# The squares of a segment's last states: one operation in place of two, and a strided read on TensorE

## The chip, the cores and the metric

The kernel runs on one NeuronCore of one Trainium2 chip. The metric is the device time of one execution in microseconds (us), taken over several runs; the median counts. The engines are named as the profile names them: PE (TensorE), DVE (VectorE), ACT (ScalarE), POOL (GpSimd) and SP (SyncE, here only an issuer of DMAs).

## What is computed

A block of two layers over x of shape (8, 512, 128): a state space layer (a recurrence over 512 time steps) and a mixture of experts. Only the recurrence touches the change. For each batch b, inner channel d (256) and state n (16):

```
def step(h, inp):
    dA_t, dB_t, x_t, C_t, t = inp
    h = h * dA_t + dB_t * x_t[:, :, None]
    nrm = jnp.sqrt(jnp.sum(h * h, axis=(1, 2), keepdims=True))
    fac = jnp.minimum(20.0 / (nrm + 1e-08), 1.0)
    h = jnp.where(t % 10 == 0, h * fac, h)
    y = jnp.einsum('bdn,bn->bd', h, C_t) + D_param * x_t
    return (h, y)
```

Every tenth step the state of a batch is scaled down if its norm, taken over all channels and states of that batch, is over 20. So the recurrence falls into segments of 10 steps (SEG), and between two segments stands a sum of squares over the whole state.

## The kernel before

**Layout.** The 256 channels are 2 halves of 128 partitions. A partition holds 256 rows of states (ROWS): half, then state n (together 32 values, H * NST), then batch b (8), with b innermost. A row has 11 slots (SLOT): slot 0 is the state that the segment starts from, slots 1 to 10 its ten steps. So the last state of row r lies at element 11 r + 10 of a buffer of `h`, which is a ring of three. The tile `sqb` has 256 columns in a partition for the squares of the last states. In the kernel before it is ordered batch first: 32 neighbouring columns belong to one batch.

**A segment S**, of which there are 52 (the last of 2 steps; 51 pass on a state), goes through these operations. Six segments make a window (s = 0 to 5 is the place in it); nine windows, each with side work for the windows around it (layer norm, projections, gates, the table `z` of tanh values).

- ACT, `decay` (L989): exp of the decays into PSUM, in four pieces of 82, 46, 82 and 46 rows (GRAN). Piece g + 2 reuses the PSUM of piece g, so it waits for the scan of piece g.
- POOL, `products` (L855): dB * x for the segment after this one; `c_last` (L869): product with C of the last six states of the segment before.
- DVE, `scan` (L1367): the recurrence itself, four scans, pieces of 902 and 506 elements (82 and 46 rows of 11).
- ACT, `square_last` (L999): squares of the last states in two operations. Part 0 takes rows 0 to 207 (SQROW) after the third scan, part 1 the other 48 after the fourth. Between them stands side work, mostly one or two tanh operations (`steps_tanh`, L1098).
- PE, `norm_sum` (L1699): 8 matmuls, one for a batch, with a stationary matrix of 8 columns (`sel`) and 32 moving columns of `sqb`; they add into an 8 x 32 corner of a PSUM bank. An fp32 matmul is two records in the trace, so a sum has 16.
- DVE, `take_norm` (L1335), a reduction to 8 values; POOL, `root` (L885, L887), the power -1/2; PE, `norm_spread` (L1705), which carries the 8 factors to all partitions; DVE, `restart` (L1341), which writes min(factor, 1) times the last states into slot 0 of the next segment. Only then can the first scan of the next segment run.
- DVE, `c_mult` (L1418), product with C of the first ten states; PE, `sum_y` (L1725, L1737), the sum over the states by matmuls with the identity; DVE, `gate_y` (L1352), of the segment before.

**What sets the order.** Each engine's program is written out by hand and runs in order; engines meet at semaphores. On DVE after the fourth scan stand gate_y, c_mult of four states, take_norm, c_mult of two, side work or c_mult, and restart. On ACT after the squares stand the first two decay pieces of the next segment and then tanh operations and side work up to the third piece. The semaphore `sq_done` counts squares: one at the start (L1492, by DVE), two a segment, and norm_sum k waits for 2k + 1. `square_last` part 0 also waits for the norm sum before (`nrm_done`), since it overwrites `sqb`.

Of the kernel before, what the change touches and what calls it, by code (L numbers as in the profile page):

```python
# [5 lines left out]
ALU = mybir.AluOpType  # L6
# [7 lines left out]
SEG = 10  # L14
# [7 lines left out]
RING = 3  # L22
# [13 lines left out]
def mamba_moe(nc, x, norm_w, W_in, conv_w, conv_b, W_dt, b_dt, W_B, W_C, A_log, D_param, W_out,  # L36
              residual_scale, Wg, w1, w2, out):
    B, T, DM = x.shape
    DI, NST = A_log.shape
    E, _, F = w1.shape  # L40
    H = DI // P
    RH = NST * B
    ROWS = H * RH
    NSEG = (T + SEG - 1) // SEG
# [11 lines left out]

    GRAN = [(0, 82), (82, 128), (128, 210), (210, ROWS)]
    NG = len(GRAN)
    SQROW = 208

    CP0 = 10
    CGRP = [(0, 6), (6, CP0)]
    NP = NST - CP0
# [3 lines left out]
    with ExitStack() as ctx:  # L67
        def sb(name, shape, dt=F32):
            return ctx.enter_context(nc.sbuf_tensor(name, shape, dt))

        def sem(name):
            return ctx.enter_context(nc.semaphore(name))
# [14 lines left out]
        sel = sb("sel", [P, B, B])  # L87
# [29 lines left out]
        h = sb("h", [P, RING, ROWS * SLOT])  # L117
# [4 lines left out]
        sqb = sb("sqb", [P, ROWS])  # L122
# [33 lines left out]
        ps = ctx.enter_context(nc.psum_tensor("ps", [P, 8, 512], F32))  # L156
        CBANK = (3, 4)
        YB, PA, PB = 5, 6, 7
        FCOL = H * BS
        NCOL = FCOL + B  # L160
# [5 lines left out]
        def rows(t, r):  # L166
            return t[:, r, :].rearrange("p (r c) -> p r c", c=SLOT)
# [11 lines left out]
        def region(G):  # L179

            if G % 2:
                return ps[:, 2, :]
            return ps[:, 0:2, :].rearrange("p k c -> p (k c)")

        zrow = z[:].rearrange("p (r b t) -> p r b t", r=H * NST, b=B)
        zall = z[:].rearrange("p (r t) -> p r t", t=WIN)
# [29 lines left out]
        sq_done = sem("sq_done"); nrm_done = sem("nrm_done")  # L216
# [25 lines left out]
        def place_of(S):  # L242

            return S // SPW, S % SPW
# [704 lines left out]
        def _(act):  # L949
# [7 lines left out]
            for k in range(TAPS):  # L957
                ins = act.activation(nat[:, k, :], win_n[:, 0, :], ACT.Identity, scale=conv_c[:, 0, k:k + 1])
# [17 lines left out]
            def decay(G):  # L976

                S, g = G // NG, G % NG
                w, s = place_of(S)
                if S == 0 and g < NG - 1:  # L980
                    act.wait_ge(tanh_first, g + 1)
                elif S == 0:
                    act.wait_ge(tanh_done, 1)
                elif g == 0:
                    act.wait_ge(tanh_done, 2 * w + (1 if s < HALF else 2))
                at_least(act, gscan, G - 1)
                r0, r1 = GRAN[g]
                n = LAST_STEPS - 1 if S == LS else SEG
                act.activation(region(G)[:, 0:(r1 - r0) * SLOT].rearrange("p (r c) -> p r c", c=SLOT)[:, :, 1:1 + n],  # L989
                               zall[:, r0:r1, SEG * s:SEG * s + n], ACT.Exp, scale=16.0).then_inc(exp_done, 1)  # L990

            def square_last(S, part):


                act.wait_ge(gscan, NG * S + 3 + part)
                if part == 0:
                    act.wait_ge(nrm_done, S + 1)
                r0, r1 = ((0, SQROW), (SQROW, ROWS))[part]
                act.activation(sqb[:].rearrange("p (b r) -> p r b", b=B)[:, r0 // B:r1 // B, :],  # L999
                               rows(h, S % RING)[:, r0:r1, SEG].rearrange("p (r b) -> p r b", b=B),  # L1000
                               ACT.Square).then_inc(sq_done, 1)

            def norm_x(v):
# [129 lines left out]
            for S in range(NSEG):  # L1133
                w, s = place_of(S)
                v1, v2, o = w + 1, w + 2, w - 1
                prep, ln, out_ = v1 < NWIN, v2 < NWIN, o >= 0

                if S == 0:
                    steps_tanh(0, 0, 16, 27)
                decay(NG * S + 2)  # L1140
                if S == 0:
                    steps_tanh(0, 0, 27, 32)
                decay(NG * S + 3)

                if s == 0:
                    if prep and w > 0:
                        silu_x(v1, 1)
                elif s == 1:
                    if prep:
                        half_tanh_dt(v1, 0)  # L1150
                        half_tanh_dt(v1, 1)
                elif s == 2:
                    if prep:
                        evac_bc(v1)
                    if w == 0:
                        steps_tanh(w, 1, 17, 22)
                    steps_tanh(w, 1, 28, 29)
                elif s == 3:
                    if prep:
                        tanh_gate(v1, 0)  # L1160
                        tanh_gate(v1, 1)
                    if w == NWIN - 1:
                        make_h2(o)
                    steps_tanh(v1, 0, 0, 1)
                elif s == 4:
                    if out_:
                        make_h2(o)
                elif s == 5:
                    steps_tanh(v1, 0, 24, 28)

                if S + 1 < NSEG:
                    square_last(S, 0)

                if S == 0:
                    silu_x(1, 0)
                elif s == 0:
                    steps_tanh(w, 1, 9, 10)
                elif s == 1:
                    steps_tanh(w, 1, 22, 23)
                elif s == 2:  # L1180
                    steps_tanh(w, 1, 29, 30)
                elif s == 3:
                    steps_tanh(v1, 0, 1, 3)
                elif s == 4:
                    steps_tanh(v1, 0, 14, 15)
                elif s == 5:
                    steps_tanh(v1, 0, 28, 29)

                if S + 1 < NSEG:
                    square_last(S, 1)  # L1190

                if S == 0:
                    silu_x(1, 1)
                if s == 2:
                    steps_tanh(w, 1, 30, 32)
                if s == 5:
                    steps_tanh(v1, 0, 29, 32)
                if s == 3 and ln:
                    evac_xT(v2)
                if s == (3 if w == NWIN - 1 else 4) and out_:  # L1200
                    evac_h2T(o)

                if S + 1 < NSEG:
                    decay(NG * S + 4)
                    decay(NG * S + 5)

                if S == 0:
                    steps_tanh(w, 1, 0, 12)
                elif s == 0:
                    steps_tanh(w, 1, 10, 22)  # L1210
                elif s == 1:
                    steps_tanh(w, 1, 23, 27)
                    if prep:
                        log_dt(v1)
                    steps_tanh(w, 1, 27, 28)
                    if w == 0:
                        steps_tanh(w, 1, 12, 17)
                elif s == 2:
                    if prep:
                        clamp_dt(v1)  # L1220
                    if ln:
                        norm_x(v2)
                    if prep:
                        scale_dt(v1)
                    if ln:
                        add_norm(v2)
                elif s == 3:
                    steps_tanh(v1, 0, 3, 14)
                elif s == 4:
                    steps_tanh(v1, 0, 15, 24)  # L1230
                    if ln:
                        silu_x(v2, 0)
                elif s == 5:
                    steps_tanh(v1, 1, 0, 9)
# [6 lines left out]
        def _(dve):  # L1241
# [6 lines left out]
            for q in range(2):  # L1248
                ins = dve.memset(xt[q * GRID:q * GRID + 3, :, :], 0.0)
# [196 lines left out]
            for k in range(TAPS):  # L1446
                ins = dve.tensor_scalar(nat[:, TAPS + k, :], win_n[:, 1, :], conv_c[:, 1, k:k + 1], None, ALU.mult)
# [28 lines left out]
            for G in range(2):  # L1476
                ins = dve.memset(region(G)[:, 0:(GRAN[G][1] - GRAN[G][0]) * SLOT].rearrange("p (r c) -> p r c", c=SLOT)[:, :, 0], 0.0)
# [8 lines left out]
            for hf in range(H):  # L1486
# [2 lines left out]
                                  b0b[:], ALU.mult).then_inc(pre_done, 1)  # L1489
            dve.wait_ge(pre_done, 3)  # L1490
            h_first = rows(h, 2)[:, :, 1]
            dve.tensor_tensor(sqb[:].rearrange("p (b r) -> p r b", b=B), h_first.rearrange("p (r b) -> p r b", b=B),  # L1492
                              h_first.rearrange("p (r b) -> p r b", b=B), ALU.mult).then_inc(sq_done, 1)
            make_gate(0, 0)
            make_gate(0, 1)
            take_norm(0)
# [66 lines left out]
        def _(pe):  # L1563
# [126 lines left out]

            def norm_sum(k):

                pe.wait_ge(sq_done, 2 * k + 1)
                at_least(pe, yg_done, k - 1)
                w, s = place_of(k - 1)
                if s == 5:
                    at_least(pe, lg_ready, w)
                for b in range(B):
                    ins = pe.matmul(ps[0:B, YB, NCOL:NCOL + H * NST], sel[:, b, :], sqb[:, b * H * NST:(b + 1) * H * NST],  # L1699
                                    start=(b == 0), stop=(b == B - 1))  # L1700
                ins.then_inc(nrm_done, 1)

# [42 lines left out]
            for k in range(16, 18):  # L1745
                ins = turn_w(k, nat[:, k, :])
# [129 lines left out]
```

## Time and profile before

| | us |
|---|---|
| median of 3 runs | 736.2 |
| lowest and highest | 733.01, 736.84 |
| span of the profiled execution | 732.8 |
| DVE busy in it | 579.2 (79%) |
| ACT busy in it | 581.7 (79%) |
| POOL busy in it | 591.9 (81%) |
| PE busy in it | 610.7 (83%) |

The profiled execution gives each instruction's start and duration. Its span of 732.8 us is what sums over instructions are made against; the median of the runs is 3.4 us more. The recurrence fills the span from about 36 us to about 600 us, the experts the rest. A start plus a duration is an end; durations of neighbouring instructions of an engine can overlap by about 0.1 us. In the timeline view neighbouring instructions of one line are merged (x2, x16), and idle time before them stands in brackets with what ended it.

### The profile page before, as it was taken

The page shows a single profiled execution, that of the slowest core. Times are in us where ns is not written, and L with a number is a line of the kernel's source. Part 1 is how long each engine was busy: PE and PEld are TensorE (multiplying, and loading weights), DVE is VectorE, ACT ScalarE, POOL GpSimd, SP SyncE. Part 2 cuts the span into 40 slices and gives each one's busy share as a digit, 9 for nine tenths or more (in the row PEclk, how much of TensorE's full clock was granted, in tenths as well). Part 3 has the DMA queues.
Part 4 walks back from the last instruction along what each step waited for, and adds up shares of the span by engine and source line. Part 5 has one row for each costly group of instructions (what it writes and reads, how often), then busy time and mean ns, then how long its engine had stood idle before and what let it go on. Part 6 is the DMA issues. An engine that isn't in the chain of part 4 may idle for free.

```text
span 732.8 us, 12812 instructions
## 1 busy us (share of the span) xinstructions
PE 610.7 (83%) x3988; PEld 475.9 (65%) x3988; DVE 579.2 (79%) x918; ACT 581.7 (79%) x1218; POOL 591.9 (81%) x567
## 2 busy tenths in 40 slices
PE   6698989889979889998988999898878794289774
PEld 4346667757757667766766766776667783179764
DVE  5577799899889989998998999889898982843221
ACT  4899989999998999999999999999988731233330
POOL 4488889999998989999998999998798860177774
PEclk9889899999989999999999999999988887589998
DMA  5341423245145313614542271244215202147561
GB/s 159 117 157 36 146 80 117 62 143 162 61 145 144 127 63 100 202 61 133 156 127 63 85 210 64 105 139 133 64 66 175 66 18 73 47 129 207 167 182 48
DMA packets 61735, 83.17 MB, mean 114 GB/s; under 512 B 14998, under 2 KB 47544, under 8 KB 61672
## 3 DMA queue, kind: packets, MB, share of 16 engines
q1 hardware_dynamic: 57896, 76.07, 34.0%
q0 software_dynamic: 2560, 6.08, 3.0%
q8 instruction: 30, 0.49, 0.3%
q10 hardware_dynamic: 1216, 0.27, 0.2%
q14 instruction: 33, 0.27, 0.1%
HBM read 69.81 MB, written 12.80 MB: 113 GB/s over the span
## 4 chain that ended last, share of the span: by engine, by line
ACT 27%; PE 22%; issue 17%; POOL 15%; DVE 13%; DMA 4%; POOLq 0%; SPq 0%; DVEq 0%; ACTq 0%
ACT z L1098 9%; POOL h L855 8%; DVE h L1367 7%; PE ps L1725 7%; ACT ps L989 7%; POOL h L869 4%; PE ps L1617 4%; DMA z<-rows_d,gidx 3%; PE ps L588 2%; PE ps L601 2%; ACT L1059 2%; ACT dtb L1059 1%; ACT xx L1016 1%; PE ps L1699 1%; ACT L1098 1%
## 5 line engine op out<-in xcount | busy, mean ns | idle before, releaser
L1367 DVE TENSOR_TENSOR_SCAN h<-ps,h 128x902 f32<-128x902 f32 x204 | 320.4, 1610 | 33.5 <-ACT ps L989 23.6
L855 POOL TENSOR_TENSOR h<-u,scr 128x640 f32<-128x640 f32 x208 | 298.2, 1462 | 2.4
L1725 PEld LDWEIGHTS ps<-h,ident 128*128 128x128 f32 x1632 | 239.4, 199 | 24.2 <-issue 21.8
L1725 PE MATMUL ps<-h,ident 128*128 128x160 f32 x1632 | 243.9, 310 | 3.3 <-issue 3.3
L1098 ACT ACTIVATE z<-dtb,asc 128x240 f32<-128x240 f32 x576 | 237.4, 485 | 0.3
L989 ACT ACTIVATE ps<-z 128x820 f32<-128x820 f32 (+1 forms) x208 | 138.2, 689 | 16.0 <-DVE h L1367 8.9
L869 POOL TENSOR_TENSOR h<-h,scr 128x960 f32<-128x960 f32 (+1 forms) x52 | 106.0, 2038 | 1.1 <-DVE h L1383 1.1
L1418 DVE TENSOR_TENSOR h<-h,ps 128x640 f32<-128x640 f32 (+2 forms) x169 | 106.5, 642 | 0.2
L1617 PE MATMUL ps<-xnT,wT 128*128 128x488 f32 x144 | 77.2, 652 | 0.3 <-ACT xnT L974 0.3
L1699 PE MATMUL ps<-sqb,sel 128*8 128x32 f32 x832 | 33.6, 195 | 37.6 <-ACT sqb L999 27.7
L1699 PEld LDWEIGHTS ps<-sqb,sel 128*8 128x8 f32 x832 | 27.2, 91 | 53.0 <-ACT sqb L999 45.7
L999 ACT ACTIVATE sqb<-h 128x208 f32<-128x208 f32 x102 | 44.5, 436 | 20.1 <-DVE h L1367 14.4
L1705 PEld LDWEIGHTS ps<-ident,fac 8*128 8x128 f32 x104 | 16.2, 194 | 54.1 <-POOL fac L887 52.6
L885 POOL TENSOR_TENSOR nrm<-s,guard 8x1 f32<-8x1 f32 x52 | 9.9, 190 | 46.9 <-DVE s L1335 46.9
L365 POOL DMA_INDIRECT z<-rows_d,gidx x32 | 33.2, 1039 | 15.6 <-issue 7.0
L373 POOL DMA_INDIRECT out_dram<-z,sidx x32 | 32.0, 1001 | 11.1 <-issue 9.5
L1705 PE MATMUL ps<-ident,fac 8*128 8x8 f32 x104 | 21.0, 271 | 21.8 <-POOL fac L887 20.8
L513 DVE TENSOR_SCALAR h<-ps 128x512 f32<-128x512 f32 x16 | 11.1, 692 | 35.3 <-PE ps L588 35.3
L1617 PEld LDWEIGHTS ps<-xnT,wT 128*128 128x128 f32 x144 | 26.1, 207 | 19.8 <-issue 19.2
L1341 DVE SCALAR_TENSOR_TENSOR h<-ps,h 128x256 f32<-128x256 f32 x52 | 32.0, 615 | 7.7 <-PE ps L1705 5.3
L887 POOL TENSOR_TENSOR fac<-nrm,neghalf_e 8x1 f32<-8x1 f32 x52 | 33.8, 650 | 4.1
L1637 PE MATMUL ps<-xc,wT 128*128 128x488 f32 x72 | 36.6, 620 | 0.0
(193 smaller groups left out, 820.2 us busy)
## 6 DMA issues: line engine op xcount, KB each, us to landing
scr<-b_d SPq DMA_DIRECT2D x52, 640.0 KB, 4.6
scr<-c_d SPq DMA_DIRECT2D x52, 240.0 KB, 4.4
z<-in_L_ffn_w_dram SPq DMA_DIRECT2D x32, 256.0 KB, 3.1
cdg<-cdg_d SPq DMA_DIRECT2D x52, 93.8 KB, 2.1
xx_d<-xx SPq DMA_DIRECT2D x8, 256.0 KB, 2.0
xxr<-xx_d SPq DMA_DIRECT2D x8, 256.0 KB, 2.8
rows_d<-h2b SPq DMA_DIRECT2D x16, 120.0 KB, 2.0
rows_d<-xxr SPq DMA_DIRECT2D x16, 120.0 KB, 2.3
```

The source lines that it names most:

```text
L855: pool.tensor_tensor(o.rearrange("p (n b) t -> p n b t", b=B), us.unsqueeze(1).to_broadcast([P, nn, B, SEG]), bb[:, S % RING, n0 * BS:(n0 ...
L869: pool.tensor_tensor(m, m, cc4[:, S % RING, :].rearrange("p (r t) -> p r t", t=SEG)[:, :, 0:n] .unsqueeze(1).to_broadcast([P, H, NP * B, n ...
L989: act.activation(region(G)[:, 0:(r1 - r0) * SLOT].rearrange("p (r c) -> p r c", c=SLOT)[:, :, 1:1 + n], zall[:, r0:r1, SEG * s:SEG * s + n ...
L999: act.activation(sqb[:].rearrange("p (b r) -> p r b", b=B)[:, r0 // B:r1 // B, :], rows(h, S % RING)[:, r0:r1, SEG].rearrange("p (r b) -> ...
L1098: ins = act.activation(zrow[:, k, :, t0:t1], dtb[:, v % 2, hf, :].rearrange("p (b c) -> p b c", b=B)[:, :, 1 + t0:1 + t1], ACT.Tanh, scale ...
L1367: dve.tensor_tensor_scan(hs, region(G)[:, 0:(r1 - r0) * SLOT], hs, 0.0, ALU.mult, ALU.add).then_inc(gscan, 1)
L1418: dve.tensor_tensor(m, m, ps[:, bk, c0:c0 + (n1 - n0) * BS].rearrange("p (r t) -> p r t", t=SEG)[:, :, 0:n] .unsqueeze(1).to_broadcast([P, ...
L1617: ins = pe.matmul(bankc((PA, PB)[hf]), wT[:, hf * TAPS + k, :], xnT[:, :, k:k + COLS], start=(k == 0), stop=(k == TAPS - 1))
L1637: ins = pe.matmul(bankc((PA, PB)[hf]), wT[:, 10 + hf * H + ih, :], xc[:, v % 3, ih, :], start=(ih == 0), stop=(ih == H - 1))
L1699: ins = pe.matmul(ps[0:B, YB, NCOL:NCOL + H * NST], sel[:, b, :], sqb[:, b * H * NST:(b + 1) * H * NST], start=(b == 0), stop=(b == B - 1))
L1705: pe.matmul(ps[:, YB, FCOL:FCOL + B], fac8[:, 0:1].to_broadcast([B, P]), ident[0:B, 0:B], start=True, stop=True).then_inc(fac_done, 1)
L1725: pe.matmul(ps[:, YB, 0:H * BS], ident[:], hr[:, :, n * B:(n + 1) * B, 0:SEG], start=(n == 0), stop=False)
```

## The change

`square_last` becomes one ACT operation over all 256 rows, after the fourth scan. It writes `sqb` in the order of the rows (half, state, batch), densely, in place of batch first. DVE's first square (L1492) writes in the same order. PE's `norm_sum` reads for each batch 32 columns that lie 8 elements (32 bytes) apart, in place of 32 neighbours. The semaphore count follows: one square a segment.

```
-            def square_last(S, part):
-
-
-                act.wait_ge(gscan, NG * S + 3 + part)
-                if part == 0:
-                    act.wait_ge(nrm_done, S + 1)
-                r0, r1 = ((0, SQROW), (SQROW, ROWS))[part]
-                act.activation(sqb[:].rearrange("p (b r) -> p r b", b=B)[:, r0 // B:r1 // B, :],
-                               rows(h, S % RING)[:, r0:r1, SEG].rearrange("p (r b) -> p r b", b=B),
+            def square_last(S):
+
+                act.wait_ge(gscan, NG * (S + 1))
+                act.wait_ge(nrm_done, S + 1)
+                act.activation(sqb[:], rows(h, S % RING)[:, :, SEG],
                                ACT.Square).then_inc(sq_done, 1)
...
-                if S + 1 < NSEG:
-                    square_last(S, 0)
-
...
                 if S + 1 < NSEG:
-                    square_last(S, 1)
+                    square_last(S)
...
-            dve.tensor_tensor(sqb[:].rearrange("p (b r) -> p r b", b=B), h_first.rearrange("p (r b) -> p r b", b=B),
-                              h_first.rearrange("p (r b) -> p r b", b=B), ALU.mult).then_inc(sq_done, 1)
+            dve.tensor_tensor(sqb[:], h_first, h_first, ALU.mult).then_inc(sq_done, 1)
...
-                pe.wait_ge(sq_done, 2 * k + 1)
+                pe.wait_ge(sq_done, k + 1)
...
-                    ins = pe.matmul(ps[0:B, YB, NCOL:NCOL + H * NST], sel[:, b, :], sqb[:, b * H * NST:(b + 1) * H * NST],
+                    ins = pe.matmul(ps[0:B, YB, NCOL:NCOL + H * NST], sel[:, b, :], sq_b[:, b, :],
                                     start=(b == 0), stop=(b == B - 1))
```

with `sq_b = sqb[:].rearrange("p (r b) -> p b r", b=B)`, batch first as a view of the dense tile.

How the instructions stand on ACT, in segment 5 (s = 5, the end of the first window): from the last tanh operations before the squares to the two decay pieces of the next segment. Before:

```order
L1098 ACTIVATE z<-dtb,asc 128x8x30 x4
L999 ACTIVATE sqb<-h 128x26x8
L1098 ACTIVATE z<-dtb,asc 128x8x30
L999 ACTIVATE sqb<-h 128x6x8
L1098 ACTIVATE z<-dtb,asc 128x8x30 x3
L989 ACTIVATE ps<-z 128x82x10
L989 ACTIVATE ps<-z 128x46x10
```

After:

```order
L1094 ACTIVATE z<-dtb,asc 128x8x30 x5
L996 ACTIVATE sqb<-h 128x256
L1094 ACTIVATE z<-dtb,asc 128x8x30 x3
L989 ACTIVATE ps<-z 128x82x10
L989 ACTIVATE ps<-z 128x46x10
```

The tanh operation that stood between the squares now stands ahead of them, and the 208 squares that were taken ahead of the fourth scan's end are taken behind it.

The same on ACT in a segment with s = 3, where the evacuation of a transpose (L974) stands between the squares and the decay pieces. Before:

```order
L1098 ACTIVATE z<-dtb,asc 128x8x30
L999 ACTIVATE sqb<-h 128x26x8
L1098 ACTIVATE z<-dtb,asc 128x8x30 x2
L999 ACTIVATE sqb<-h 128x6x8
L974 COPY xnT<-ps 128x512
L989 ACTIVATE ps<-z 128x82x10
L989 ACTIVATE ps<-z 128x46x10
```

After:

```order
L1094 ACTIVATE z<-dtb,asc 128x8x30 x3
L996 ACTIVATE sqb<-h 128x256
L974 COPY xnT<-ps 128x512
L989 ACTIVATE ps<-z 128x82x10
L989 ACTIVATE ps<-z 128x46x10
```

Again nothing but the squares has changed its place among the others. On PE, DVE and POOL every instruction stands where it stood; only what PE reads and what the waits count is different.

## Rows read from the trace of the kernel before

**Rows 1.** The page: busy us of each engine, share of the span, instructions.

```profile
PE 610.7 (83%) x3988; PEld 475.9 (65%) x3988; DVE 579.2 (79%) x918; ACT 581.7 (79%) x1218; POOL 591.9 (81%) x567
```

**Rows 2.** Stretch, its us, busy PE, PEld, DVE, ACT, POOL, granted clock, DMA share, GB/s.

```profile
110.00:583.00 473.00, 421.43 (x2877) 329.34 (x2877) 434.14 (x596) 446.32 (x925) 433.45 (x398) 0.96 0.38 115
```

**Rows 3.** Groups by form: out<-in, count, busy us, mean ns, idle before.

```profile
L989 ACT ACTIVATE ps<-z 128x820 f32<-128x820 f32 x102 | 86.5, 848 | 6.1 <-DVE h L1367 5.4
...
L1418 DVE TENSOR_TENSOR h<-h,ps 128x640 f32<-128x640 f32 x88 | 71.0, 807 | 0.1
L989 ACT ACTIVATE ps<-z 128x460 f32<-128x460 f32 x102 | 55.7, 546 | 3.8 <-DVE h L1367 3.5
...
L1418 DVE TENSOR_TENSOR h<-h,ps 128x320 f32<-128x320 f32 x79 | 34.9, 467 | 0.0
...
L999 ACT ACTIVATE sqb<-h 128x208 f32<-128x208 f32 x51 | 29.8, 584 | 12.4 <-DVE h L1367 11.8
...
L999 ACT ACTIVATE sqb<-h 128x48 f32<-128x48 f32 x51 | 14.8, 289 | 7.7 <-DVE h L1367 2.6
```

**Rows 4.** The same view: DVE operations that read or write with a long stride.

```profile
L1487 DVE TENSOR_TENSOR h<-u,b0b 128x128 f32<-128x128 f32 x2 | 0.6, 383 | 0.0
...
L1378 DVE TENSOR_TENSOR sqb<-h,ps 128x82 f32<-128x82 f32 x2 | 0.6, 296 | 0.3 <-ACT ps L989 0.2
...
L1378 DVE TENSOR_TENSOR sqb<-h,ps 128x46 f32<-128x46 f32 x2 | 0.4, 222 | 0.0
```

**Rows 5.** Timeline (start us, us, engine line), one segment's end, s = 1.

```profile
321.97 1.19 DVE L1367 TENSOR_TENSOR_SCAN h<-ps,h 128x506 f32<-128x506 f32 x1
322.57 0.48 ACT L1098 ACTIVATE z<-dtb,asc 128x240 f32<-128x240 f32 x1
...
323.19 0.29 ACT L999 ACTIVATE sqb<-h 128x48 f32<-128x48 f32 x1
323.29 0.81 DVE L1418 TENSOR_TENSOR h<-h,ps 128x640 f32<-128x640 f32 x1
323.38 1.31 ACT L989 ACTIVATE ps<-z 128x820 f32<-128x820 f32 x2
...
323.53 0.63 PE L1699 MATMUL ps<-sqb,sel 128*8 128x32 f32 x16 [0.43 <-ACT sqb L999]
...
324.20 0.18 DVE L1335 TENSOR_REDUCE s<-ps 8x1 f32<-8x32 f32 x1
...
324.46 0.18 POOL L885 TENSOR_TENSOR nrm<-s,guard 8x1 f32<-8x1 f32 x1 [1.11 <-DVE s L1335]
...
325.31 0.38 PE L1705 MATMUL ps<-ident,fac 8*128 8x8 f32 x2
...
325.73 0.62 DVE L1341 SCALAR_TENSOR_TENSOR h<-ps,h 128x256 f32<-128x256 f32 x1 [0.16 <-PE ps L1705]
...
326.48 3.14 DVE L1367 TENSOR_TENSOR_SCAN h<-ps,h 128x902 f32<-128x902 f32 x2
326.55 4.51 PE L1725 MATMUL ps<-h,ident 128*128 128x160 f32 x32
```

**Rows 6.** Timeline, the third scan in segments with s = 2, 3 and 4.

```profile
331.27 3.14 DVE L1367 TENSOR_TENSOR_SCAN h<-ps,h 128x902 f32<-128x902 f32 x2 [1.65 <-ACT ps L989]
...
342.81 2.04 DVE L1367 TENSOR_TENSOR_SCAN h<-ps,h 128x902 f32<-128x902 f32 x1 [0.35 <-ACT ps L989]
...
353.61 3.14 DVE L1367 TENSOR_TENSOR_SCAN h<-ps,h 128x902 f32<-128x902 f32 x2 [0.36 <-ACT ps L989]
```

**Rows 7.** Waits: us in total, times, longest us.

```profile
ACT sqb L999 <- DVE h L1367: 14.4, 34, 1.6
...
DVE s L1335 <- PE ps L1699: 5.8, 7, 1.9
```

**Rows 8.** Timeline, the segment with s = 2 of the first window.

```profile
72.59 0.55 ACT L999 ACTIVATE sqb<-h 128x208 f32<-128x208 f32 x1
...
74.42 0.18 DVE L1335 TENSOR_REDUCE s<-ps 8x1 f32<-8x32 f32 x1 [1.63 <-PE ps L1699]
```

More of the change, by code:

```diff
@@ L58, in mamba_moe @@
     NG = len(GRAN)
-    SQROW = 208
     CP0 = 10
@@ L183, in region @@
             return ps[:, 0:2, :].rearrange("p k c -> p (k c)")
+        sq_b = sqb[:].rearrange("p (r b) -> p b r", b=B)
         zrow = z[:].rearrange("p (r b t) -> p r b t", r=H * NST, b=B)
```

## The prediction, made before the changed kernel ran

> **What bounds the kernel now.** I read the busy times first. Over the whole span no engine passes 83% [rows 1], but in the stretch from 110 to 583 us, which holds most of the recurrence, DVE, ACT, POOL and PE are all busy for 89 to 94% of 473 us [rows 2], and PE has its higher clock (granted 0.96 of 2.4 GHz). With four engines that full, busy time says little; what counts is who waits for whom between two segments. So next comes the timeline around one boundary [rows 5]. The fourth scan ends at 321.97 + 1.19 = 323.16. From there:
>
> ACT's small square 323.19 to 323.48; PE's norm sum 323.53 to 324.16; DVE's reduction at 324.20; POOL's root from 324.46; PE's spread 325.31 to 325.69; DVE's restart at 325.73, after an idle 0.16 us that ended with the spread; next first scan at 326.48.
>
> DVE is not idle in between: its c_mult of four states runs from 323.29 to 324.10. So it is free 0.10 us before the sum is there. The chain square, sum, reduction and DVE's own work are matched almost to the tenth, and the reduction stands in DVE's queue ahead of the rest of c_mult, of the restart and thus of the next scan. Whatever makes the sum later makes DVE later by the same amount. The wait view agrees: only seven reductions wait noticeably longer, 5.8 us in all [rows 7].
>
> The first square, of 208 rows, is not on this path. It is taken while the fourth scan runs. ACT is early for it: it idles 12.4 us before the 51 large squares and 7.7 us before the small ones [rows 3], in 34 cases plainly waiting for a scan [rows 7].
>
> ACT is the other pacer. Where s is 2, 3 and 4 the third scan waits for an exp piece, by 1.65, 0.35 and 0.36 us [rows 6]; ACT's program from the square to that piece is then what lasts longest. In the other three kinds of segment no such wait of any size stands in the timeline.
>
> **Change 1: one square in place of two.** Before, 584 + 289 = 873 ns [rows 3]. The two sizes give a slope of (584 - 289) / 160 = 1.84 ns an element and a constant of 200 ns. The exp pieces on the same engine, whose neighbours lie in runs, have (848 - 546) / 360 = 0.84 ns. So the squares pay a full nanosecond an element for a stride. Two strides are there: the read at 44 bytes, which stays, and the write at 128 bytes, which goes. Which of them costs, ACT's rows can't say; DVE's can. Its usual product costs (807 - 467) / 320 = 1.06 ns an element plus 127 ns [rows 3]. L1378 reads at 44 bytes and writes densely: (296 - 222) / 36 = 2.06 ns. L1487 reads in runs and writes at 44 bytes: (383 - 127) / 128 = 2.0 ns [rows 4]. One stride alone, of either sort, already doubles the price. So the dense write should win little, and I take 200 + 256 x 1.84 = 671 ns. The ends: 200 + 256 x 0.84 = 415 ns if on ACT the write was the whole trouble, 873 ns if merging saves nothing.
>
> The merged square starts where the small one started, 0.03 us behind the fourth scan, and so ends 671 - 289 = 0.38 us later. On ACT the tanh operation of 0.48 us that stood between the squares [rows 5] moves ahead, into time in which ACT is now idle. ACT saves 202 ns of work but can't use them: the saving is a longer wait for the scan. What stands behind the square, the decay pieces and all up to the third piece, is 0.38 us late.
>
> The Trainium skill, "Advanced Engine Details and Errata", section "The Read-Write Bubble", advises large operations on ScalarE and VectorE, since memory latency shows as a bubble between instructions. The 200 ns that a merge saves agree with it; what the rule would make of the time is the last rival below.
>
> **Change 2: PE reads with a stride of 32 bytes.** Sixteen records take 0.63 us [rows 5]; with 193 ns for a single one they stand (0.63 - 0.19) / 15 = 29 ns apart. The state sum streams 160 columns a record, 32 records in 4.51 us, or 135 ns each [rows 5], which is 0.85 ns a column; for 32 columns that is 27 ns. So the norm sum is paced by its moving columns, not by issue, and a slower read shows in full. No matmul of the trace reads single fp32 elements with a gap. Bounds: nothing, or four times (each element fetched anew for each half pass): 16 x 0.081, about 1.25 us. Nearest are DVE's and ACT's rows, where an element with a gap costs twice one in a run; I take that, 16 x 0.027 = 0.42 us. A gain is excluded, since a dense read is the least that can be asked.
>
> The rule that speaks against this change: the Trainium skill, "Advanced Engine Details and Errata", section "SBUF Cachelines", says that SBUF has 16-byte lines, that at least two hits on a line are needed to hide the latency, and that an access to a new line each time pays. By it both strides here pay, as DVE's rows show; it gives no figure for PE.
>
> DVE's first square, once, is strided on one side instead of two: nothing. The counts on `sq_done` cost nothing. The merged square's wait for the last norm sum is met long before.
>
> **The sum.** The sum's end is late by D = 0.38 + 0.42 = 0.80 us, DVE's reduction by 0.79. How much of it is still there when the third scan of the next segment starts depends on who was waited for. Into s = 2 DVE had waited 1.65 us for ACT, so DVE's lateness is covered and ACT's own 0.38 is left. Into s = 3 and 4 the covers are 0.35 and 0.36: 0.44 and 0.43 are left. Into s = 5, 0 and 1 there is next to no cover; for two of them I take off 0.15, the idle time before the restart [rows 5], which POOL's root can hide where it was late for its own reasons: 0.79 + 0.64 + 0.64. Together 0.38 + 0.44 + 0.43 + 2.07 = 3.3 us a window, 0.55 a segment. Of the 51 segments I count 45. In some at the start, around 220 us and at the end the sum was late for another reason (PE's queue, or ACT not yet there), as in [rows 8], where the large square starts only at 72.59 and DVE then idles 1.63 us; there ACT's saved 0.2 us is even of use. 45 x 0.55 = 25 us. The profiled execution would go from 732.8 to 758; with the 3.4 us by which the median lies above it, **761 us**.
>
> PE's own 51 x 0.42 = 21 us of extra streaming are in time in which it waits for squares or roots. If that cover were gone, gate_y would wait for sum_y; I count nothing.
>
> **Rivals.**
> - PE reads the strided columns for nothing. Then both engines are 0.38 late at every boundary: 45 x 0.38 = 17, 753 us. For it: PE's records may hide a fetch that DVE can't. Chance 0.28.
> - PE's read costs four times: D = 1.63. Left are 0.38 + 1.28 + 1.27 + 1.63 + 1.48 + 1.48 = 7.5 a window, 45 x 1.25 = 56: 792 us. Chance 0.08.
> - The write stride was ACT's price, PE's read costs double: the square takes 415 ns, so ACT is 0.13 late and D is 0.55. Left: 0.13 + 0.20 + 0.19 + 0.55 + 0.40 + 0.40 = 1.9 a window, 14 in all: 750 us. Against it stand L1378 and L1487. Chance 0.09.
> - Both cheap, 415 ns and nothing on PE: 45 x 0.13 = 6, 742 us, or hardly slower at all if the constant shrinks to that of exp (160 ns) and the early segments give some back. Chance 0.06.
> - The other side: ACT's work, not its wait, sets the pace. Then 202 ns a segment come off, 51 x 0.20 = 10, 726 us. It decides only where ACT reaches the square after the fourth scan's end; [rows 3, 7] show ACT waiting, [rows 8] is one of the few exceptions. This is also what the skill's advice on large operations would bring. Chance 0.02.
>
> **How the numbers follow.** The forecast has 0.45, its own range about 754 to 767 (45 to 51 segments, covers off by a tenth). With the first and third rivals 0.82 of the chance lies between 745 and 768. What is left over, 0.02, is for something not seen. About 0.5%, 3.7 us, is what a measurement of this kernel can tell from no change: faster 0.02, same 0.04, slower 0.94.
>
> **What would show it.** The squares' row: 51 operations of 128x256, mean near 671 ns (415 would be the write stride). The norm sum's 16 records: 1.05 us (0.63: PE reads for nothing; 1.9: four times). From the fourth scan's end to the reduction 1.85 us in place of 1.04, with DVE idle about 0.9 us before it, some 45 us in all over the reductions. The third scan's waits for ACT in s = 3 and 4 nearly gone, in s = 2 about 1.2 us. ACT's idle before the squares some 0.6 us each. I am wrong if the reduction doesn't idle, or if segments with s = 2 grow as much as those with s = 5.

## The result, and the profile after

The changed kernel takes 765.8 us (median of 4 runs, 763.5 to 771.1); the kernel before, measured beside it again, 735.1. The ratio is 1.044, with a 95% interval of 1.039 to 1.048. The profiled execution went from 732.8 to 761.8 us, 29 us more.

The page: busy time of each engine in the changed kernel, to be read against [rows 1]. ACT and DVE are busy for less, PE for 34 us more, and the span is longer: the time went into waiting.

```profile
span 761.8 us, 12761 instructions
...
PE 644.3 (85%) x3988; PEld 499.9 (66%) x3988; DVE 576.8 (76%) x918; ACT 575.2 (76%) x1167; POOL 592.8 (78%) x567
```

The view of groups by form says where DVE waits (last columns: busy us, mean ns, idle us before them and what ended it). The functions are those of the kernel before, their lines a few lower: scan L1360, norm_sum L1691, square_last L996, gate_y L1345, take_norm L1328.

```profile
L1360 DVE TENSOR_TENSOR_SCAN h<-ps,h 128x902 f32<-128x902 f32 x102 | 206.6, 2026 | 20.6 <-ACT ps L989 11.7 <-POOL h L855 1.6 <-DVE h L1334 1.0
...
L1691 PE MATMUL ps<-sqb,sel 128*8 128x32 f32 x832 | 58.2, 238 | 36.0 <-ACT sqb L996 29.6 <-DVE sqb L1485 4.9 <-DVE yg L1345 0.8
...
L996 ACT ACTIVATE sqb<-h 128x256 f32<-128x256 f32 x51 | 33.7, 660 | 41.6 <-DVE h L1360 41.5
...
L1345 DVE TENSOR_TENSOR yg<-ps,sgn 128x160 f32<-128x160 f32 x51 | 15.7, 308 | 15.9 <-PE ps L1729 15.9
...
L1328 DVE TENSOR_REDUCE s<-ps 8x1 f32<-8x32 f32 x52 | 9.3, 178 | 46.0 <-PE ps L1691 45.9
```

And the same groups of the kernel before, of which the rows ahead of the prediction show only the squares.

```profile
L1367 DVE TENSOR_TENSOR_SCAN h<-ps,h 128x902 f32<-128x902 f32 x102 | 207.4, 2033 | 33.0 <-ACT ps L989 23.0 <-POOL h L855 1.6 <-DVE h L1341 1.0
...
L1699 PE MATMUL ps<-sqb,sel 128*8 128x32 f32 x832 | 33.6, 195 | 37.6 <-ACT sqb L999 27.7 <-DVE sqb L1492 4.9 <-DVE lgb L1441 4.7
...
L1352 DVE TENSOR_TENSOR yg<-ps,sgn 128x160 f32<-128x160 f32 x51 | 15.5, 305 | 8.2 <-PE ps L1737 8.2
...
L1335 DVE TENSOR_REDUCE s<-ps 8x1 f32<-8x32 f32 x52 | 9.3, 179 | 9.8 <-PE ps L1699 5.8
```

DVE idles 46.0 - 9.8 = 36.2 us longer before the reduction of the norm sum (of the 9.8 us before, 5.8 ended with PE's sum) and 15.9 - 8.2 = 7.7 us longer for the state sum, and 33.0 - 20.6 = 12.4 us less before its large scans, nearly all of it waits for ACT's exp pieces. Together 31.5, against a span that grew by 29 while DVE's busy time shrank by 2.4.

One boundary, the counterpart of [rows 5] (timeline, s = 1). The fourth scan ends at 335.56 + 3.11 = 338.67.

```profile
335.56 3.11 DVE L1360 TENSOR_TENSOR_SCAN h<-ps,h 128x902 f32<-128x902 f32 x2
...
338.71 0.66 ACT L996 ACTIVATE sqb<-h 128x256 f32<-128x256 f32 x1 [0.94 <-DVE h L1360]
338.81 0.81 DVE L1411 TENSOR_TENSOR h<-h,ps 128x640 f32<-128x640 f32 x1
...
339.42 1.12 PE L1691 MATMUL ps<-sqb,sel 128*8 128x32 f32 x16 [0.66 <-ACT sqb L996]
...
340.57 0.18 DVE L1328 TENSOR_REDUCE s<-ps 8x1 f32<-8x32 f32 x1 [0.96 <-PE ps L1691]
...
342.10 0.61 DVE L1334 SCALAR_TENSOR_TENSOR h<-ps,h 128x256 f32<-128x256 f32 x1 [0.16 <-PE ps L1697]
...
342.84 3.14 DVE L1360 TENSOR_TENSOR_SCAN h<-ps,h 128x902 f32<-128x902 f32 x2
...
347.17 3.14 DVE L1360 TENSOR_TENSOR_SCAN h<-ps,h 128x902 f32<-128x902 f32 x2 [1.19 <-ACT ps L989]
```

From the end of the scan to the reduction it is 1.90 us, where it was 1.04: the square 0.37 longer (660 ns for 289), PE's sixteen records 0.49 longer (1.12 for 0.63). DVE's c_mult ends at 339.62 and DVE then stands for 0.96 us. The restart follows the reduction by 1.53 us, as before. The third scan of the next segment (347.17), which waited 1.65 us for ACT [rows 6], waits 1.19.

From first scan to first scan, the growth of a segment in two neighbouring windows, in us:

| s | 0 | 1 | 2 | 3 | 4 | 5 | sum |
|---|---|---|---|---|---|---|---|
| segments 24 to 29 | 1.50 | 0.70 | 0.39 | 0.39 | 0.39 | 0.55 | 3.9 |
| segments 30 to 35 | 0.90 | 1.03 | 0.04 | 0.38 | 0.38 | 0.69 | 3.4 |

Segments with s = 2, 3 and 4 grow by ACT's 0.38 in both windows (once by 0.04, where the segment before took the rest). The others grow by more, and by an amount that changes from window to window; that had to be explained.

### The profile page after: what moved, and what is told of

Its sections match the earlier page's. It is cut to its first block, busy times and chain, and to the rows that moved or that the text cites. A ratio compares the mean times of both kernels' runs of the same rounds, so it can differ in the third digit from the quotient of the medians.

```text
span 761.8 us, 12761 instructions
## 1 busy us (share of the span) xinstructions
PE 644.3 (85%) x3988; PEld 499.9 (66%) x3988; DVE 576.8 (76%) x918; ACT 575.2 (76%) x1167; POOL 592.8 (78%) x567
## 4 chain that ended last, share of the span: by engine, by line
PE 32%; DVE 27%; issue 17%; ACT 12%; POOL 6%; DMA 3%; DVEq 0%; POOLq 0%; SPq 0%; ACTq 0%
DVE h L1360 15%; PE ps L1717 10%; PE ps L1691 6%; PE ps L1609 4%; DVE h L1411 3%; ACT sqb L996 3%; PE ps L1629 2%; ACT z L1094 2%; POOL fac L887 2%; ACT ps L989 2%; DVE h L1334 2%; POOL out_dram L373 2%; DMA z<-rows_d,gidx 2%; DVE bst L1260 2%; PE ps L1697 1%
## 5 line engine op out<-in xcount | busy, mean ns | idle before, releaser
L1360 DVE TENSOR_TENSOR_SCAN h<-ps,h 128x902 f32<-128x902 f32 x204 | 317.1, 1606 | 21.1 <-ACT ps L989 12.3
L1717 PEld LDWEIGHTS ps<-h,ident 128*128 128x128 f32 x1632 | 239.1, 199 | 27.2 <-issue 23.9
L1094 ACT ACTIVATE z<-dtb,asc 128x240 f32<-128x240 f32 x576 | 235.0, 485 | 0.3
L989 ACT ACTIVATE ps<-z 128x820 f32<-128x820 f32 (+1 forms) x208 | 139.9, 692 | 33.6 <-DVE h L1360 26.0
L1691 PE MATMUL ps<-sqb,sel 128*8 128x32 f32 x832 | 58.2, 238 | 36.0 <-ACT sqb L996 29.6
L1691 PEld LDWEIGHTS ps<-sqb,sel 128*8 128x8 f32 x832 | 48.7, 105 | 51.1 <-ACT sqb L996 41.9
L1609 PE MATMUL ps<-xnT,wT 128*128 128x488 f32 x144 | 79.3, 667 | 0.3 <-ACT xnT L974 0.3
L996 ACT ACTIVATE sqb<-h 128x256 f32<-128x256 f32 x51 | 33.7, 660 | 41.6 <-DVE h L1360 41.5
L1328 DVE TENSOR_REDUCE s<-ps 8x1 f32<-8x32 f32 x52 | 9.3, 178 | 46.0 <-PE ps L1691 45.9
L1629 PE MATMUL ps<-xc,wT 128*128 128x488 f32 x72 | 43.2, 714 | 0.4 <-DVE xc L1317 0.4
```

The source lines that it names most:

```text
L996: act.activation(sqb[:], rows(h, S % RING)[:, :, SEG], ACT.Square).then_inc(sq_done, 1)
L1094: ins = act.activation(zrow[:, k, :, t0:t1], dtb[:, v % 2, hf, :].rearrange("p (b c) -> p b c", b=B)[:, :, 1 + t0:1 + t1], ACT.Tanh, scale ...
L1360: dve.tensor_tensor_scan(hs, region(G)[:, 0:(r1 - r0) * SLOT], hs, 0.0, ALU.mult, ALU.add).then_inc(gscan, 1)
L1609: ins = pe.matmul(bankc((PA, PB)[hf]), wT[:, hf * TAPS + k, :], xnT[:, :, k:k + COLS], start=(k == 0), stop=(k == TAPS - 1))
L1629: ins = pe.matmul(bankc((PA, PB)[hf]), wT[:, 10 + hf * H + ih, :], xc[:, v % 3, ih, :], start=(ih == 0), stop=(ih == H - 1))
L1717: pe.matmul(ps[:, YB, 0:H * BS], ident[:], hr[:, :, n * B:(n + 1) * B, 0:SEG], start=(n == 0), stop=False)
```

## The experiments

The theory: two losses of their own, ACT's square (later for the sum and for ACT itself) and PE's strided read (later for the sum), each partly covered by the other's or by older waits. Rivals: all is PE's read; all is the merge; the two only hurt together. All ratios are to runs of the kernel before on the same chip; the chips differ by up to 2% (before: 731.7, 734.7 and 747.9 us in the three groups of runs), so only ratios are compared.

**1. Each part alone.** `merge_only`: one square, but layout and reads as before.

```
+                act.activation(sqb[:].rearrange("p (b r) -> p r b", b=B),
+                               rows(h, S % RING)[:, :, SEG].rearrange("p (r b) -> p r b", b=B), ACT.Square)
```

> Part one of the change alone: one square of 256 rows after the fourth scan, but written batch first as before, and PE reads 32 neighbours as before. Own theory (a merged square makes the boundary late whatever PE does): square about 670 ns, the norm sum's 16 records in 0.63 us, the sum 0.38 us later after the fourth scan than before, ACT late by the same, 45 x 0.38 = 17 us: about 752 us. If all the loss were in PE's strided read: as before, 735 us. If ACT's saved 0.2 us a segment counted: 725 us.

Measured: ratio 1.034 (1.031 to 1.037), 757.3 against 731.7 us. That is 25.6 us, half as much again as expected. `stride_only`: two squares at their places, written in the order of the rows, PE's strided read.

```
-                act.activation(sqb[:].rearrange("p (b r) -> p r b", b=B)[:, r0 // B:r1 // B, :],
-                               rows(h, S % RING)[:, r0:r1, SEG].rearrange("p (r b) -> p r b", b=B),
+                act.activation(sqb[:, r0:r1], rows(h, S % RING)[:, r0:r1, SEG],
```

> Part two alone: two squares at their old places, written densely in the order of the rows, and PE reads with a stride of 32 bytes. Own theory: 238 ns a record and 1.12 us a sum as in the changed kernel, so DVE's reduction 0.49 us late, ACT not late; covered in segments with s = 2, partly in s = 3 and 4 by scans that wait for ACT (0.35 us): 0 + 0.14 + 0.13 + 0.49 + 0.34 + 0.34 = 1.4 us a window, 12 us in all: about 747 us. If the merge were all of the loss: 735 us. If the two losses only hurt together (each covered alone): both this and the merge alone near 735 us.

Measured: 1.020 (1.017 to 1.023), 746.6 against 731.7, 14.9 us. Groups by form, first of the merge alone, then of the stride alone:

```profile
L1361 DVE TENSOR_TENSOR_SCAN h<-ps,h 128x902 f32<-128x902 f32 x102 | 207.2, 2032 | 34.7 <-ACT ps L989 25.3 <-POOL h L855 1.6 <-DVE h L1335 1.0
...
L996 ACT ACTIVATE sqb<-h 128x256 f32<-128x256 f32 x51 | 34.0, 667 | 48.1 <-DVE h L1361 47.9
...
L1346 DVE TENSOR_TENSOR yg<-ps,sgn 128x160 f32<-128x160 f32 x51 | 15.6, 307 | 15.7 <-PE ps L1731 15.7
...
L1329 DVE TENSOR_REDUCE s<-ps 8x1 f32<-8x32 f32 x52 | 9.3, 179 | 22.2 <-PE ps L1693 22.1
```

```profile
L1368 DVE TENSOR_TENSOR_SCAN h<-ps,h 128x902 f32<-128x902 f32 x102 | 206.8, 2027 | 23.3 <-ACT ps L991 14.4 <-POOL h L857 1.6 <-DVE h L1342 1.0
L1699 PE MATMUL ps<-sqb,sel 128*8 128x32 f32 x832 | 58.1, 238 | 25.1 <-ACT sqb L1001 16.5 <-DVE sqb L1493 4.9 <-DVE lgb L1442 3.0
...
L1336 DVE TENSOR_REDUCE s<-ps 8x1 f32<-8x32 f32 x52 | 9.3, 179 | 33.7 <-PE ps L1699 33.6
```

Both parts hurt alone, so the three rivals fall. With the merge alone the waits before the large scans stay about as long as they were (33.0 and 34.7 us), since DVE and ACT are late together. With the stride alone DVE is late and ACT is not, and they shrink to 23.3 us: part of the later sum is covered by older waits for ACT.

The parts add up to 40 us on that chip, and the change costs 4.4%, 31 to 32 us. That doesn't mean that one hides the other at the boundary, as a look at whole windows shows. Six segments last, from first scan to first scan (start of the first scan of segment 18, 24, 30 and 36), in us; in brackets gate_y's waits for the state sum in them that are over 0.15 us:

| | segments 18 to 23 | 24 to 29 | 30 to 35 |
|---|---|---|---|
| before | 64.56 | 64.56 | 64.56 |
| stride_only | 65.48 | 66.98 (0.77) | 65.48 |
| merge_only | 66.78 | 68.35 (1.50) | 68.35 (1.42) |
| act_late (experiment 3) | 66.53 | 66.72 (0.82) | 66.38 |
| merge_filled (experiment 4) | 68.86 (0.78) | 68.56 (0.49) | 66.89 |
| changed kernel | 68.89 (1.36) | 68.47 (1.10) | 67.98 (0.59) |
| after_filled (experiment 4) | 67.65 | 67.66 | 67.63 |

The lines behind two of these numbers, the windows of the merge alone from 246.66 and from 313.44 us:

```profile
246.66 2.04 DVE L1361 TENSOR_TENSOR_SCAN h<-ps,h 128x902 f32<-128x902 f32 x1
...
313.44 2.04 DVE L1361 TENSOR_TENSOR_SCAN h<-ps,h 128x902 f32<-128x902 f32 x1
...
320.97 0.33 DVE L1346 TENSOR_TENSOR yg<-ps,sgn 128x160 f32<-128x160 f32 x1 [1.08 <-PE ps L1731]
...
381.79 2.04 DVE L1361 TENSOR_TENSOR_SCAN h<-ps,h 128x902 f32<-128x902 f32 x1
```

Where gate_y doesn't wait, the stride costs 0.9 us a window, the merge 2.2 (six times 0.37) and both together 3.1: there the parts simply add up. What is not additive lies in the windows in which gate_y waits. These waits grow by 2.6 us over the span with the stride (8.2 to 10.8), by 7.5 with the merge and by 7.7 with both. That accounts for 2.4 of the missing 8 to 9 us; the rest isn't explained, and one profiled execution of each kernel doesn't tell how often such windows come in the others.

**2. Which stride costs, and from what distance.** `merge_dense_read` is the changed kernel with PE reading 32 neighbours; `read_stride_8B` and `read_stride_16B` read every second and every fourth column; `blocks_of_4` lays the squares out so that a batch has four neighbouring columns in each block of 32.

```
-                    ... sel[:, b, :], sq_b[:, b, :],
+ merge_dense_read   ... sel[:, b, :], sqb[:, b * H * NST:(b + 1) * H * NST],
+ read_stride_8B     ... sel[:, b, :], sqb[:, 0:2 * H * NST].rearrange("p (r two) -> p r two", two=2)[:, :, b % 2],
+ read_stride_16B    ... sel[:, b, :], sqb[:, 0:4 * H * NST].rearrange("p (r four) -> p r four", four=4)[:, :, b % 4],
+ blocks_of_4        ... sel[:, b, :], sqb[:].rearrange("p (q b i) -> p b q i", b=B, i=4)[:, b],
```

> The changed kernel, but PE reads 32 neighbouring columns of the row-ordered squares (so each sum takes the wrong squares, the norm is not the reference's). Against the merge alone it differs only in ACT's write, dense in place of 128 bytes apart. If the read stride alone sets ACT's price: the same square and the same time as the merge alone, within 0.3%. If a write stride adds its own price to it: square shorter here by up to 0.26 us (415 ns) and some 11 us less. PE's sum 0.63 us.

> The changed kernel, but PE reads every second column (8 bytes apart) from the first 64 (the norm is not the reference's). If the price of PE's read is one per 16-byte line with fewer than two hits: two hits a line, no price, sum 0.63 us and the time of the merge with a dense read (about 752 us). If any gap between single elements doubles the price: 1.12 us and the changed kernel's 766 us.

> The changed kernel, but PE reads every fourth column (16 bytes apart) from the first 128 (the norm is not the reference's). Theory of lines (one element in a 16-byte line costs double): 238 ns a record, 1.12 us a sum, 766 us (ratio 1.04) as with 32 bytes. If the price grew with the distance or came from the bank: between 193 and 238 ns.

> The changed kernel with another layout of the squares: blocks of 32 in which a batch has 4 neighbouring columns (one line of 16 bytes). ACT writes elements 16 bytes apart in one operation, PE reads runs of 4 with 112 bytes between the runs. Theory of lines: PE pays nothing (193 ns, 0.63 us), ACT pays no more than for its read (square 660 to 671 ns), so the time of the merge alone, ratio 1.034. If any jump cost PE something, the sum would be over 0.63 us.

| | distance of PE's columns | ns a record | ACT's square, mean ns | ratio (95%) |
|---|---|---|---|---|
| merge_only | 4 B | 195 | 667 | 1.034 (1.031 to 1.037) |
| merge_dense_read | 4 B | 195 | 660 | 1.034 (1.028 to 1.039) |
| read_stride_8B | 8 B | 194 | 660 | 1.033 (1.028 to 1.038) |
| blocks_of_4 | runs of 4, then 112 B | 195 | 675 | 1.031 (1.027 to 1.035) |
| read_stride_16B | 16 B | 237 | 660 | 1.041 (1.038 to 1.044) |
| changed kernel | 32 B | 238 | 660 | 1.044 (1.039 to 1.048) |

The norm sum of segments with s = 1, in the timeline of 8 bytes, then of 16 bytes:

```profile
331.34 0.64 PE L1691 MATMUL ps<-sqb,sel 128*8 128x32 f32 x16 [0.67 <-ACT sqb L996]
```

```profile
341.20 1.12 PE L1691 MATMUL ps<-sqb,sel 128*8 128x32 f32 x16 [0.67 <-ACT sqb L996]
```

PE's price is a step: nothing at 8 bytes, double at 16, the same double at 32, and nothing for jumps of 112 bytes between runs of four. That is what a price for having a single element in a line of 16 bytes would give; a distance of 12 bytes and other alignments were not tried. Here the rule of the Trainium skill ("Advanced Engine Details and Errata", "SBUF Cachelines": at least two hits on a 16-byte line) and the trace agree, for PE also, on which the page gives no figure: (1.12 - 0.24) / 15 = 59 ns between records of 32 columns, 29 before.

On ACT the write stride is worth 7 ns of 667, so it is not what the squares pay for. That leaves the read at 44 bytes; no run reads the squares densely, so its own price stays argued. With the order of the rows the change therefore buys ACT next to nothing and charges PE 0.49 us a segment.

**3. Is it ACT or the sum that the merge makes late?** `act_late` is the kernel before with an ACT operation on a scratch tile behind the small square (it takes 400 ns).

```
                     square_last(S, 1)
+                    act.activation(junk[:], wT[:, 0:2, :].rearrange("p k c -> p (k c)"), ACT.Identity)
```

> The kernel before with an ACT operation of 256 columns on a scratch tile right behind the small square, about 0.38 us, with no one waiting for it: ACT is as late as with the merged square, while the norm sum comes at its old time. If ACT's lateness is half of the merge's loss: growth where scans wait for ACT (s = 2, 3, 4: 0.38 us each, 45 / 6 x 1.14 = 9 us, 741 us where before is 732, ratio 1.012). If only the late sum hurts: 732 us, 1.00. If the clock falls less often here than with the merge, s = 0 and s = 3 stay without their extra 0.7 us and more.

Measured: 1.018 (1.014 to 1.021), 12.4 us, of which I had expected 9. Groups by form:

```profile
L1369 DVE TENSOR_TENSOR_SCAN h<-ps,h 128x902 f32<-128x902 f32 x102 | 207.5, 2034 | 44.8 <-ACT ps L990 35.8 <-POOL h L856 1.6 <-DVE h L1343 1.0
...
L1354 DVE TENSOR_TENSOR yg<-ps,sgn 128x160 f32<-128x160 f32 x51 | 15.6, 305 | 8.3 <-PE ps L1739 8.1
...
L1337 DVE TENSOR_REDUCE s<-ps 8x1 f32<-8x32 f32 x52 | 9.3, 179 | 9.8 <-PE ps L1701 5.9
```

All of it is in the wait for exp pieces (33.0 to 44.8 us); the reductions wait 9.8 us as ever. The added operation makes ACT late by less than its 400 ns, as the timeline of a segment with s = 1 shows:

```profile
327.47 0.29 ACT L1000 ACTIVATE sqb<-h 128x48 f32<-128x48 f32 x1
...
327.67 0.40 ACT L1192 ACTIVATE junk<-wT 128x256 f32<-128x256 f32 x1
...
327.97 1.31 ACT L990 ACTIVATE ps<-z 128x820 f32<-128x820 f32 x2
```

From the small square to the decay piece it is 0.50 us, where it was 0.19 [rows 5]: ACT is 0.31 us late, where the merge makes it 0.37 late. For that an undisturbed window pays 66.53 - 64.56 = 1.97 us and 1.82 in the next but one (table above), six times 0.30 to 0.33. So ACT's path was about last in all six kinds of segment, not in three. (In the kernel before the third scan waits for ACT by 0.02 to 0.10 us where s is 5, 0 and 1.) ACT's lateness is by itself enough for the 2.2 us that the merge costs an undisturbed window, while DVE's later sum runs beside it. In whole executions the run costs half of the merge, 12.4 of 25.6 us; the difference is mostly in windows in which gate_y waits.

**4. Why the merge costs 25 us and not 17.** Seven and a half windows (45 segments) at 2.2 us would be the 17 us that were expected. The rest is in windows in which gate_y waits: 68.35 us in place of 66.78 for the merge, where gate_y waits for 1.50. In the windows in which s = 0 grew most, PE is slow just ahead of the late gate_y. Timeline of the changed kernel around segment 24, and under it the view of stretches (the granted clock is the third number from the end):

```profile
319.97 2.00 PE L1609 MATMUL ps<-xnT,wT 128*128 128x488 f32 x2
...
321.76 1.55 PE L1629 MATMUL ps<-xc,wT 128*128 128x488 f32 x2
...
328.10 0.32 DVE L1345 TENSOR_TENSOR yg<-ps,sgn 128x160 f32<-128x160 f32 x1 [1.10 <-PE ps L1729]
```

```profile
319.50:322.90 3.40, 3.40 (x6) 1.95 (x7) 2.92 (x4) 3.18 (x10) 3.24 (x4) 0.50 0.88 232
322.90:326.30 3.40, 3.40 (x25) 3.16 (x25) 3.40 (x3) 2.94 (x5) 3.40 (x3) 1.00 0.40 119
```

The same two pairs of matmuls took 1.09 and 0.98 us before. Between 319.5 and 322.9 us the granted clock was 0.50 (the lower level, 1.2 GHz), after PE had waited 0.72 us for the square and 0.38 for the root. The state sum starts late and gate_y stands for 1.10 us. In the kernel before PE waits just as long at this place, 0.68 and 0.38 us, and the granted clock of the stretch from 305.4 to 308.8 us, which holds the same matmuls, is 1.00; so these two waits alone don't tell why the clock fell. Between 110 and 560 us the trace of the kernel before has 7 such stretches, that of the merge alone 10 (the expectation below says 6 and 12, a miscount), and in the kernel before four of the seven begin at the end of a segment with s = 2 (272, 337, 402 and 467 us), where gate_y doesn't wait. `merge_filled` gives PE a matmul nobody needs ahead of the norm sum; `after_filled` and `before_filled` do it to the changed kernel and to the kernel before.

```
+                if s != 1 and w < NWIN - 1 and S > 2:
+                    pe.matmul(ps[:, CBANK[1], 0:256], ones_w[:], wT[:, 0:2, :].rearrange("p k c -> p (k c)"),
+                              start=True, stop=True)
                 norm_sum(S + 1)
```

> The merge alone plus a matmul of 256 columns (about 0.45 us) on PE right ahead of the norm sum, into a free PSUM bank, in all segments from the fourth on but s = 1 and the last window; its result isn't used. With the merge alone PE's clock is at its lower level in 12 stretches between 110 and 560 us, in the kernel before in 6, and segments with s = 0 and s = 3 grow by 1.2 and 1.0 us in place of 0.4 in the windows in which the clock falls. If these falls are PE's longer idle times and cost time: fewer lower stretches and about 7 us less than the merge alone (ratio 1.024). If the extra growth has another cause: the ratio stays 1.034 or goes up, since the filler delays the sum where PE is not idle for 0.45 us.

> The changed kernel plus the same filler on PE ahead of the norm sum (256 columns, about 0.45 us, result unused). The filler took about 8 us (1.1%) off the merge alone. In the changed kernel the waits of gate_y for the state sum (15.9 us against 8.2 before) stood where PE's clock had fallen. If the fallen clock makes them: gate_y's waits near 10 us, and a ratio to before of about 1.034 in place of 1.044. If PE is simply too full with the slower reads: the filler adds work, 1.044 or more.

> The kernel before plus the same filler. There PE idles only 0.4 to 1.0 us ahead of the sum, so the filler delays the sum a little where the idle time is shorter than 0.45 us. If the clock's falls in the kernel before (granted 0.97 between 110 and 560 us) cost anything on the path: up to 3 us faster, ratio 0.996. If they lie where PE has time to spare: 1.000 to 1.003.

| | ratio without filler | with filler | gate_y's waits, us | granted clock, 110 to 560 us |
|---|---|---|---|---|
| merge | 1.034 (1.031 to 1.037) | 1.023 (1.020 to 1.027) | 15.7, 10.3 | 0.96, 0.97 |
| changed kernel | 1.044 (1.039 to 1.048) | 1.034 (1.028 to 1.039) | 15.9, 10.4 | 0.94, 0.97 |
| before | 1 | 0.999 (0.996 to 1.002) | 8.2, 8.4 | 0.97, 0.98 |

Groups by form of the changed kernel with filler:

```profile
L1345 DVE TENSOR_TENSOR yg<-ps,sgn 128x160 f32<-128x160 f32 x51 | 15.5, 304 | 10.4 <-PE ps L1729 10.3
...
L1328 DVE TENSOR_REDUCE s<-ps 8x1 f32<-8x32 f32 x52 | 9.3, 179 | 51.1 <-PE ps L1691 51.0
```

And the stretch of 450 us in it; below it the same stretch of the changed kernel without filler and of the kernel before:

```profile
110.00:560.00 450.00, 421.47 (x2689) 323.06 (x2688) 389.96 (x547) 402.54 (x799) 393.42 (x362) 0.97 0.37 111
```

```profile
110.00:560.00 450.00, 416.18 (x2605) 316.50 (x2605) 388.03 (x539) 402.12 (x798) 390.31 (x360) 0.94 0.36 110
```

```profile
110.00:560.00 450.00, 402.37 (x2745) 311.90 (x2745) 413.71 (x571) 427.32 (x883) 413.69 (x383) 0.97 0.38 117
```

The filler makes the reductions wait some 5 us longer and still takes 1% off by the ratios, in both kernels with the merged square. In the kernel before it does nothing that can be measured. How many us that is, is less sure. By the medians the change costs 30.7 us without filler and 28.1 with it (776.1 against 747.9), and the merge 25.6 and 18.8; but `merge_dense_read`, `read_stride_8B` and `blocks_of_4`, in which PE's records and ACT's square take the merge's times within 8 ns, cost 24.5, 23.9 and 22.3 us. So the filler gives back something between 3 and 8 us. Its effect on gate_y's waits is overstated by the pair 15.7 and 10.3 too, for these three kernels have 11.1, 12.2 and 12.8 us without any filler. The windows point the same way and give a second estimate: without gate_y's waits the changed kernel grows by 3.1 us a window, 23 us in 45 segments, and its profiled execution grew by 29, so some 6 us are in windows in which gate_y waits.

What is shown is that PE runs at half clock ahead of such a wait (the lines above), and that with the filler stretches at the lower level are fewer between 110 and 560 us: 5 in place of 13 in the changed kernel, 6 in place of 10 with the merge. What makes the clock fall is not shown. More waiting of PE is not enough of an account: ahead of its norm sums PE idles 37.6 us in the kernel before, 36.0 in the changed kernel, whose granted clock is lower, and 47.6 in `act_late`, which has seven stretches at the lower level like the kernel before.

No version came out ahead of the kernel before.

## Why the prediction was right, step by step

The forecast was 761 us within 745 to 768; measured 765.8. For the profiled execution 758 was expected and 761.8 measured.

- **The balance at the boundary.** Right: with the sum 0.86 us later, DVE idles 0.96 us at the reduction, and the restart keeps its distance of 1.53 us. The idle time over the reductions was forecast at about 45 us and came out at 46.0.
- **The square.** 671 ns forecast, 660 measured. That a write stride adds next to nothing to the read stride was argued from DVE; `merge_only` against `merge_dense_read` (667 and 660) shows it on ACT itself. The argument from L1378 was weaker than it looked: that operation reads two operands at 44 bytes, one in SBUF and one in PSUM, and not one alone.
- **PE's read.** Double, 0.42 us, was taken between nothing and 1.25 us; measured double, 0.49 us. The method (the price of an element with a gap on the other engines) held, and the step between 8 and 16 bytes shows on PE what a rule of lines would give.
- **ACT's covers.** Right in sign, a little short in size: into s = 3 and 4 the waits of 0.35 us vanish and the segments grow by 0.38; into s = 2 a wait of 1.19 is left (1.2 forecast). Of a window the forecast was 3.3 us. Undisturbed windows, which only the changed kernel with filler has, grow by 3.1, and the two above, with gate_y's waits in them, by 3.9 and 3.4. Wrong was that ACT's path is the last only where s is 2, 3 and 4: `act_late` shows it level with DVE's in all six. For the sum this changes nothing, since DVE is later than ACT here.
- **"If that cover were gone, gate_y would wait for sum_y; I count nothing."** This step failed. The term was put at nothing and measured 7.7 us more of gate_y's waiting (15.9 against 8.2). Ahead of the wait that was followed up PE ran at half clock, and with the filler the waits are 10.4 us. What makes the clock fall stays open. The prediction said of the clock only that it was high.
- **The sum.** Forecast 25 us, measured 29 in the profiled execution. By the undisturbed windows 45 segments cost 45 / 6 x 3.1 = 23 us, 2 under the forecast: the covers hid a little more than I gave them. The other 6 are an estimate of what gate_y's waits added, and nothing in the forecast stood for them. So the hit is partly two errors against each other, though the first is small.
- **Rivals.** PE's reading for nothing (753 us) is refuted for this stride. At 8 bytes PE does read for nothing, and even so that kernel is 3.3% slower than the kernel before, 24 us and not the 17 of this rival. The rival that ACT's work sets the pace is refuted: ACT saved 6.5 us of busy time and idled 21.5 us more before its squares (41.6 against 12.4 + 7.7).

## What to carry to other kernels

A reduction that two engines wait for should be cut so that only its smallest part is taken after the last producer; merging it saves issue time on an engine that is waiting anyway and puts the whole operation on the path. A layout that makes the writer's pattern simple moves the stride to the reader: look at who reads, how often, and whether the reader is paced by its data; here a reader at 8 bytes (two fp32 to a line of 16 bytes) or in runs of four paid nothing. And when a cost changes from one window to the next, look at PE's granted clock and at what PE does at that place, not only at the waits that the edit was meant to change.

## What the runs showed of the hardware that I had not expected

- PE's fp32 read has a sharp step between 8 and 16 bytes (194 and 237 ns a record of 32 columns, 0.64 and 1.12 us for sixteen), and no further one at 32 bytes (238 ns).
- On ACT strides of read and write don't add: 256 elements read at 44 bytes take 660 ns with a dense write, 667 with a write at 128 bytes, 675 at 16 bytes.
- A matmul whose result is thrown away (256 columns, in most segments) made two kernels faster, by 1% in the ratios and 3 to 8 us by the runs taken together, and left a third as it was. The mean granted clock between 110 and 560 us was 0.97 with it and 0.94 and 0.96 without.
- The granted clock can be lower where PE is busier: in the changed kernel PE is busy for 416.2 of the 450 us at 0.94, in the kernel before for 402.4 at 0.97. Part of that busy time is made by the lower clock and the slower reads themselves.
